# Preparation stage in groups of ten row tiles: normalisation on GpSimd, scaled values kept in PSUM

## The reference, cut to what matters

```python
x = ctx_1024                       # (1, 6404, 128)
latents = _layernorm(x_tokens)     # (1, 1024, 128), plain layer norm
x   = layer_norm(x, ln_m_g, ln_m_b)          # mean, var over the 128 columns, gain and bias
lat = layer_norm(latents, ln_l_g, ln_l_b)    # a second layer norm on the first
kv_input = concatenate([x, lat], axis=1)     # 7428 rows
q = lat @ Wq;  k, v = split(kv_input @ Wkv)  # 16 heads of 64
out = softmax(q k^T / 8) v @ Wout
```

## Time and profile before

| What | us |
|---|---|
| Median of 3 runs | 2458.1 (2455.87 to 2459.36) |
| The profiled execution's own time | 2455.94 |
| Its span, first to last instruction | 2454.1 |
| PE / DVE / ACT / POOL busy in the span | 2297.6 / 1862.8 / 1673.8 / 1848.4 |
| Longest single group: POOL L631 (attention) | 1767.0 |
| First instruction of the attention stage | 62.83 |

### The profile page before, as it was taken

How to read it: one execution, slowest core, us unless ns; L and a number is a source line. 1 busy time by engine, 2 the same in 40 slices (tenths; PEclk the granted TensorE clock), 3 DMA queues, 4 the chain that set the end, 5 groups by cost and what they waited for, 6 DMA issues and landing times. The chain is left out here.

```text
span 2454.1 us, 68499 instructions
## 1 busy us (share of the span) xinstructions
PE 2297.6 (94%) x27961; PEld 1491.5 (61%) x27961; DVE 1862.8 (76%) x2822; ACT 1673.8 (68%) x3037; POOL 1848.4 (75%) x1105
## 2 busy tenths in 40 slices
PE   2999999999999999999999999999999998679986
PEld 1365665666566656665666566656665566558874
DVE  8878888887888788888888788888887751467754
ACT  4677777777777777777777777777777775256642
POOL 1798898889888988898889988998899997120000
PEclk9999999999999999999999999999999998889988
DMA  2431324132413241324132413141313000700000
GB/s 88 118 85 46 85 69 116 44 87 69 114 44 89 69 112 44 91 67 114 43 92 63 118 43 93 62 119 43 93 61 90 2 2 10 193 6 2 2 4 10
DMA packets 124490, 165.61 MB, mean 67 GB/s; under 512 B 26376, under 2 KB 100048, under 8 KB 123728
## 3 DMA queue, kind: packets, MB, share of 16 engines
q1 hardware_dynamic: 120880, 157.13, 22.6%
q10 hardware_dynamic: 3296, 4.10, 0.6%
HBM read 99.22 MB, written 61.97 MB: 66 GB/s over the span
## 5 line engine op out<-in xcount | busy, mean ns | idle before, releaser
L631 POOL TENSOR_TENSOR att_prob_low<-att_prob 128x1024 f16<-128x1024 f32 x960 | 1767.0, 1867 | 190.5 <-PE all_banks L751 151.4
L908 ACT ACTIVATE att_prob<-all_banks 128x512 f32<-128x512 f32 x1888 | 1070.7, 591 | 386.1 <-PE all_banks L716 262.9
L1002 DVE TENSOR_REDUCE att_part<-all_banks 128x2 f32<-128x1024 f32 x800 | 946.7, 1218 | 194.9 <-PE all_banks L676 194.9
L737 PE MATMUL all_banks<-att_v,att_prob 128*128 128x129 f16 x5664 | 583.5, 220 | 2.8 <-DVE shared_att L1026 0.6
L737 PEld LDWEIGHTS all_banks<-att_v,att_prob 128*128 128x128 bf16 x5664 | 414.1, 98 | 237.5 <-issue 10.1
L751 PEld LDWEIGHTS all_banks<-att_v,att_prob_low 128*128 128x128 f16 x7552 | 328.6, 98 | 135.4 <-POOL att_prob_low L631 15.9
L697 PE MATMUL all_banks<-att_qc,att_kc 128*128 128x512 f16 x1056 | 401.1, 380 | 0.0
L698 PE MATMUL all_banks<-att_qd,att_kd 128*128 128x512 f16 x1056 | 400.8, 380 | 0.0
L751 PE MATMUL all_banks<-att_v,att_prob_low 128*128 128x65 f16 x7552 | 385.0, 194 | 11.4 <-POOL att_prob_low L631 11.3
L741 PE MATMUL all_banks<-att_v,att_prob 128*128 128x64 f16 x1888 | 371.1, 197 | 0.0
L739 PE MATMUL all_banks<-att_v,att_prob 128*128 128x65 f16 x1888 | 365.7, 194 | 0.0
(11 more groups left out here) (304 smaller groups left out, 3076.6 us busy)
## 6 DMA issues: line engine op xcount, KB each, us to landing
v_all<-att_stage_v SPq DMA_DIRECT2D x98, 258.0 KB, 2.5
att_kc<-k_high SPq DMA_DIRECT2D x90, 232.0 KB, 3.9
att_v<-v_all SPq DMA_DIRECT2D x28, 483.8 KB
att_v<-v_all SPq DMA_DIRECT2D x28, 451.5 KB
k_high<-att_stage_h SPq DMA_DIRECT2D x98, 128.0 KB, 1.7
k_low<-att_stage_l SPq DMA_DIRECT2D x98, 128.0 KB, 1.9
att_kd<-k_low SPq DMA_DIRECT2D x45, 232.0 KB, 4.2
att_kc<-k_high SPq DMA_DIRECT2D x30, 232.5 KB, 4.6
```

The costliest lines, as they stand in the source:

```text
L631: pool.tensor_tensor(prob_low[g % NL][:, 0:w], p[:, 0:w], p.bitcast(BF16)[:, 1:2 * w:2], op=ALU.subtract).then_inc(low_split, 1)
L737: pe.matmul(O[:, q, :], w, v[:, e, t, :], start=first, stop=False, skip_group_check=True)
L908: act.activation(prob[g % NP][:, i * BANK:(i + 1) * BANK], S[n % 3], ACT.Exp, scale=SCALE)\
L1002: dve.tensor_reduce(parts[:, n:n + 2], pers.banks[:, 4 + 2 * pair:6 + 2 * pair, :], axis=AX.X, op=ALU.max)\
```

## The change

Only `stage_prepare` changes. The work is cut into the five groups in which the context arrives, plus the tail.

1. The 59 `normalize` operations of L139 that feed the transposes move from DVE to POOL, in the order of the tiles; POOL waits for `rstd_ready` before each group. The low parts of the weights come behind them on POOL.
2. DVE computes the reciprocal deviation group by group (`group_rstd`): statistics of group n + 1, then reciprocal deviation of group n, then the low parts of the chunks of group n - 1.
3. ACT scales the transposed tile in its PSUM bank in place, waits for itself, and copies the bank's whole width to `kvh`. The f32 buffer `full` in SBUF is gone; DVE subtracts `kvh` from the PSUM bank.
4. There are 8 banks `T` instead of 4, and a bank is free again when its low part has been taken (`low_ready`), not when its high part has.
5. ACT's square roots stand between the chunks: that of group n + 2 behind the chunks of group n. The weights' high parts come behind the square root of group 2.

```diff
-        NF = 4
-        full = sc.sb("full", [P, NF, BANK])
+        NF = 8
...
+            def group_std(n):
+                if n < CL:
+                    norm_sqrt(act, nk, n * PER, (n + 1) * PER, n + 1)
+                else:
+                    norm_sqrt(act, nk, CTX_TILES, CTX_TILES + 1, CL + 1, TAIL)
+            def parts_of(c):
                 act.wait_ge(transposed, c + 1)
-                if c >= NF:
-                    act.wait_ge(low_ready, c - NF + 1)
...
-                    last = act.activation(full[:, c % NF, o0:o1], T[c % NF][:, o0:o1], ACT.Identity, bias=b, scale=g)
-                    if o1 == w:
-                        last.then_inc(full_ready, 1)
-                    last = act.activation(kvh[:, c * BANK + o0:c * BANK + o1], T[c % NF][:, o0:o1], ACT.Identity,
-                                          bias=b, scale=g)
-                    if o1 == w:
-                        last.then_inc(high_ready, 1)
+                    last = act.activation(T[c % NF][:, o0:o1], T[c % NF][:, o0:o1], ACT.Identity, bias=b, scale=g)
+                last.then_inc(full_ready, 1)
+                act.wait_ge(full_ready, c + 1)
+                act.activation(kvh[:, c * BANK:c * BANK + w], T[c % NF][:, 0:w], ACT.Copy).then_inc(high_ready, 1)
+
+            group_std(0)
+            group_std(1)
+            act.wait_ge(g_in, 64)
+            for n in range(CL - 1):
+                for c in range(n * PER // 4, (n + 1) * PER // 4):
+                    parts_of(c)
+                group_std(n + 2)
+                if n == 0:
+                    act.wait_ge(w_in, 32)
...
+            for c in range((CL - 1) * PER // 4, K_CHUNKS):
+                parts_of(c)
...
         @block.gpsimd
+            for n in range(CL):
+                pool.wait_ge(rstd_ready, n + 1)
+                for t in range(n * PER, (n + 1) * PER):
+                    normalize(pool, ctx[:, t, :], ctx[:, t, :], nk, t).then_inc(tile_ready, 1)
+            for t in range(TOKEN_TILES):
+                normalize(pool, lat[:, t, :], lat[:, t, :], nl, t).then_inc(tile_ready, 1)
+            pool.wait_ge(rstd_ready, CL + 1)
+            normalize(pool, tail[:, :], tail[:, :], nk, CTX_TILES, TAIL).then_inc(tile_ready, 1)
...
         @block.vector
+            def group_rstd(n):
+                lo, hi, rows = (n * PER, (n + 1) * PER, P) if n < CL else (CTX_TILES, CTX_TILES + 1, TAIL)
+                std, var, r, a = (t[0:rows, lo:hi] for t in (nk.std, nk.var, nk.rstd, nk.a))
+                dve.wait_ge(nk.std_ready, n + 1)
+                steps.link(dve.reciprocal(r, std))
...
+                dve.tensor_tensor(r, r, a, op=ALU.mult).then_inc(rstd_ready, 1)
             def low_parts(c):
-                dve.wait_ge(full_ready, c + 1)
                 dve.wait_ge(high_ready, c + 1)
-                dve.tensor_tensor(kvl[:, k], full[:, c % NF, 0:width(c)], kvh[:, k], op=ALU.subtract)
+                dve.tensor_tensor(kvl[:, k], T[c % NF][:, 0:width(c)], kvh[:, k], op=ALU.subtract).then_inc(low_ready, 1)
+            group_stats(0)
+            for n in range(CL):
+                group_stats(n + 1)
+                group_rstd(n)
+                if n:
+                    for c in range((n - 1) * PER // 4, n * PER // 4):
+                        low_parts(c)
+            group_rstd(CL)
+            for c in range((CL - 1) * PER // 4, K_CHUNKS):
+                low_parts(c)
...
         @block.tensor
                 if c >= NF:
-                    pe.wait_ge(high_ready, c - NF + 1)
+                    pe.wait_ge(low_ready, c - NF + 1)
```

More of the change, by code:

```diff
@@ L172, in stage_prepare @@
         vec, tile_ready, transposed = sc.sem("vec"), sc.sem("tile_ready"), sc.sem("transposed")
+        rstd_ready = sc.sem("rstd_ready")
         full_ready, high_ready, low_ready = sc.sem("full_ready"), sc.sem("high_ready"), sc.sem("low_ready")
@@ L229, in _ @@
                     g, b = gains[:, kind:kind + 1], gains[:, kind + 1:kind + 2]
-                    last = act.activation(full[:, c % NF, o0:o1], T[c % NF][:, o0:o1], ACT.Identity, bias=b, scale=g)
-                    if o1 == w:
-                        last.then_inc(full_ready, 1)
-                    last = act.activation(kvh[:, c * BANK + o0:c * BANK + o1], T[c % NF][:, o0:o1], ACT.Identity,
-                                          bias=b, scale=g)
-                    if o1 == w:
-                        last.then_inc(high_ready, 1)
+                    last = act.activation(T[c % NF][:, o0:o1], T[c % NF][:, o0:o1], ACT.Identity, bias=b, scale=g)
[11 more added lines that the diff above has]
+                    act.wait_ge(w_in, 32)
+                    act.activation(pers.wk_h[:, :], wkv[:, 0:INNER], ACT.Copy).then_inc(w_high, 1)
+                    act.activation(pers.wq_h[:, :], wq[:, :], ACT.Copy).then_inc(w_high, 1)
+                    act.activation(pers.wv_h[:, :], wkv[:, INNER:2 * INNER], ACT.Copy).then_inc(w_high, 1)
+            for c in range((CL - 1) * PER // 4, K_CHUNKS):
+                parts_of(c)
         @block.gpsimd
@@ L267, in _, with group_stats @@
             norm_rstd(dve, steps, nl, 0, TOKEN_TILES, 1)
-            for n in range(CL):
+            def group_stats(n):
+                if n == CL:
+                    dve.wait_ge(tail_in, 16)
+                    steps.link(dve.bn_stats(nk.stats[0:TAIL, CTX_TILES, :], tail[:, :]))
+                    norm_moments(dve, steps, nk, CTX_TILES, CTX_TILES + 1, TAIL)
+                    return
                 dve.wait_ge(ctx_in[n], 16)
@@ L273, in _ @@
                 norm_moments(dve, steps, nk, n * PER, (n + 1) * PER)
[L274 to L278, removed]
+            def group_rstd(n):
[3 more added lines that the diff above has]
+                steps.link(dve.reciprocal(r, std))
+                steps.link(dve.tensor_tensor(a, r, r, op=ALU.mult))
+                steps.link(dve.tensor_tensor(a, a, var, op=ALU.mult))
+                steps.link(dve.tensor_scalar(a, a, -0.5, 1.5, ALU.mult, ALU.add))
+                dve.tensor_tensor(r, r, a, op=ALU.mult).then_inc(rstd_ready, 1)
@@ L298, in _ @@
-            low_parts(K_CHUNKS - 2)
-            low_parts(K_CHUNKS - 1)
+                dve.tensor_tensor(kvl[:, k], T[c % NF][:, 0:width(c)], kvh[:, k], op=ALU.subtract).then_inc(low_ready, 1)
[9 more added lines that the diff above has]
+                low_parts(c)
```

## The result

| | before | after |
|---|---|---|
| Median of 6 runs, us | 2457.39 (2455.87 to 2459.36) | 2469.52 (2467.43 to 2470.16) |
| Profiled execution, us | 2455.94 | 2469.51 |
| Span, us | 2454.1 | 2467.7 |
| First instruction of the attention stage, us | 62.83 | 74.50 |

The change makes the kernel slower: ratio 1.0047, 95% interval 1.0037 to 1.0058. I had forecast 2452.2, in a range up to 2463. The difference of the medians is 12.1 us, and the preparation stage ends 74.50 - 62.83 = 11.7 us later, so the loss is in the stage that was changed. That first instruction is POOL's; DVE's first one of the attention stage moves from 62.91 to 74.96, by 12.05 us. The six executions of the kernel before scatter by 3.5 us, so a profiled execution and a median agree only to a microsecond or two.

The account below looks back on a forecast made before the run. DVE was taken to bound the preparation stage, which runs alone; with tiles on POOL it would end at 22.1 + 21.2 + 7.1 + 6.3 = 56.7 us, 5.9 less, so 2452.2 us against the median, range 2447 to 2463.

Parts of the forecast that it names:

- What bounds the kernel: First 62.6 us run alone, DVE the bound; a microsecond off the preparation's last engine is one off the kernel.
- p: Preparation: time from one POOL normalisation of a 128x128 tile to the next, taken as 0.36 us.
- The sum: Preparation's end as 22.1 + 59 p + gaps + 6.3: 56.7 us against 62.55, 5.9 less.
- the gaps: POOL's waits between groups for DVE's reciprocal deviations: 7.1 us in all at p 0.36, 4.6 at 0.658.
- Rival 3: Preparation: POOL's normalisation costs more than 0.575 us a tile, kernel slower; at 0.658 it takes 2467.3 us; chance 0.17.
- ACT: Per chunk in preparation: scaling in place 0.78 us, wait for itself 0.05, then the copy, 1.33 against 1.36 before.
- The page on GpSimd: On POOL's normalisation: line rate with one input, gain near 8 us; twice DVE's pitch, 1.6 us slower; neither in forecast.
- Equal time: The price of a POOL normalisation at which the changed kernel neither gains nor loses: p = 0.49.

Follow-up runs that it names:

- The probe: Kernel before plus 19 extra POOL instructions (tensor_scalar and tensor_tensor forms, several widths) on scratch data while POOL idles; 2460.7 us in one execution, against 2456.9.
- The wide runs: Changed kernel with POOL normalising several tiles at once by two tensor_tensor operations: all tiles, 2460.7 us; six of ten tiles on DVE instead, 2465.4 us.

## Why the prediction was wrong

- **What bounds the kernel.** Right: a microsecond off or on the last engine of the preparation is one off or on the kernel. The attention stage starts 11.7 us later on POOL and 12.05 on DVE, and the medians differ by 12.1. The two profiled spans differ by 13.6; the last 1.5 us arise in later stages. PE's granted clock at the start of the attention stage is 1.00 in both, so it isn't that, and the cause stays open; the medians don't show it.
- **p.** This is the step that failed: I took 0.36 and bounded it by 0.658; it is 0.777. My bounds were rows of other operations of POOL, and the upper one counted columns of a two-input subtraction. The probe shows that this was the wrong family: at 512 columns the tensor_scalar costs 2.05 times the two-input operation (2.120 against 1.035), and its per-partition operands cost 0.15 more at 128. I argued that one tensor input must be cheaper than two; on POOL here it is dearer.
- **The sum.** The form of the sum was right, and two of its terms were off: p added 59 x (0.777 - 0.36) = 24.6 us to my 56.7, and the gaps that didn't come took 7.1 off: 22.1 + 59 x 0.777 + 0 + 6.3 = 74.2, and POOL's last operation ends at 74.19. So p is the error that decided, and the missing gaps hid a part of it. Rival 3 happened, with the mechanism named there, a tile above 0.575 us, and at a price 18% above the bound that I thought generous. I gave it 0.17.
- **The gaps.** Wrong too: none, where I had 7.1 us at p = 0.36 and 4.6 at 0.658. I let every DVE operation of these kinds wait for the end of POOL's. Rows 4 show that for POOL's tensor_tensor only. Beside POOL's tensor_scalar seven small operations from 23.97 to 24.90 keep their 0.17 to 0.19; the longest in the stage is 0.37, so each deviation is out before POOL is done with the group before. The wide runs show the waits where I expected them, because there POOL's operation is a tensor_tensor.
- **ACT.** Scaling in place 0.75 (0.78 taken), its wait for itself 26.63 - 25.85 - 0.75 = 0.03 (0.05 taken), low part 0.69 and never held up. Right.
- **The page on GpSimd.** By the Trainium skill, GPSIMD Engine Reference, section "When to use GPSIMD", one input is roughly line rate and two inputs are twice as slow as on VectorE. No row here agrees with the first half for tensor_scalar: 0.642 us for 128 columns even with immediates. A DVE normalisation has a pitch of 0.26, so at 0.777 POOL is 3.0 times as slow with one tensor input, far from line rate. The second half comes nearer: a weight's low part, two inputs, takes 2.11 us on POOL and 1.22 on DVE, 1.7 times.
- **What would have been cheap to see.** Equal time needed p below 0.49, and all rows near it were of other operations. A chance of 0.53 for faster rested on an operation that no row showed; the range should have gone further up.

## What to carry to other kernels

An engine gets work from another by its own price for that very operation: before 59 tensor_scalar operations of 128 columns move to POOL, one of them has to be timed there, because neither its memset nor its two-input rows bound it. Where the move pays, it pays in part: three of ten tiles on POOL, with POOL's tensor_tensor operations placed in the windows in which DVE takes low parts from PSUM or runs bn_stats, gave 0.9981, where all ten gave 1.0047. And what stood free beside the busy engine (6.3 us of weights here) has to be placed anew, since at the end it is bare and in a row it shuts DVE out.

## What the runs showed of the hardware that was not expected

- POOL's tensor_scalar, f32, two per-partition operands, takes 0.793 us at 128 columns, 1.224 at 256 and 2.120 at 512, on 4 rows 0.783; a two-input tensor_tensor takes 0.448 at 128 and 1.035 at 512.
- How long a DVE operation waits depends on POOL's operation: beside the normalisation's own tensor_scalar of 128 columns it loses 0 to 0.2 us, beside the probe's other tensor_scalar forms (one operand at 128 columns, or 256 and 512 columns) up to 0.46, though those of 512 columns last 2.07 to 2.23; beside tensor_tensor it lasts to the end of that (0.17 becomes 2.15 us). bn_stats keeps 2.02 us for ten beside either.
- The exclusion goes the other way as well: DVE operations of 1.22 us stretched single POOL tiles of 0.79 us to 1.62, as the view of that line gives (min, median, max in ns):

```profile
L139 POOL TENSOR_SCALAR prep_lat<-prep_lat,prep_nl_mean,prep_nl_rstd x8: 786/787/1623, 61.9 to 68.9; 128x128 f32<-128x128 f32 x8
```

- ACT can scale a PSUM bank in place at 0.75 us for 512 columns, 0.03 less than into SBUF. With a wait for its own semaphore the next pass starts 0.03 after the end of the first; without one it starts 0.10 before it (0.68 against 0.78), so the wait costs 0.13.
